# Attention and a mixture of experts on one core: the maximum pass taken in two row halves of the array, with its maxima over two banks

## The chip, the cores and the metric

The kernel runs on one core of a Trainium2 chip. The metric is the device time of one execution in microseconds (us), a median over runs. Fewer is better.

## The reference, cut to what matters

```python
# x: (1, 2048, 256), ctx: (1, 1601, 256), lenS2: the number of valid keys (at most 1601)
x = x + attention(layernorm(x), ctx, ctx, lenS2, ...)   # 16 heads of width 64, then Wo
x = x + experts(layernorm(x), gate_w, w1, w2, w3)       # 8 experts, the best 2 of each row

def attention(...):
    q_in, k_in, v_in = layer_norm(query), layer_norm(key), layer_norm(value)   # gain and bias
    q, k, v = q_in @ Wq + bq, k_in @ Wk + bk, v_in @ Wv + bv                   # 16 heads
    q, k = rope(q), rope(k)
    scores = einsum('bhqd,bhkd->bhqk', q, k) / 8
    scores = where(key < lenS2, scores, -inf)
    attn = softmax(scores)
    return einsum('bhqk,bhkd->bhqd', attn, v) @ Wo + bo
```

Everything is float32. The kernel gets near to that with bfloat16 matmuls by splitting operands into a high half (the value rounded or cut to bfloat16) and a low half (what is left).

## The kernel before

There are three stages: `prepare` (norms, transposes, splits), `attend` (the attention of the 16 heads), and `experts`. Only `attend` and constants that it uses are touched.

`attend` is compiled for 10, 11, 12 or 13 tiles of 128 keys (`KEY_TILES`) and chooses by the length at run time. In the runs here it is 10 tiles, 1280 keys: 640 exponentials over 64 blocks. `Plan(10)` sets what follows.

Two heads make a pair, and there are 8 pairs. A head's 2048 queries are 4 chunks of 512, so a pair has 8 blocks (head, chunk). A block has 5 groups of two key tiles, and the program advances in slots, one group each (`slot` on every engine; `s = 5 * block + m`).

For a head, `Q1` holds the high half of q twice (partitions 0 to 63 and 64 to 127), `K1` the high half of k on partitions 0 to 63 and its low half on 64 to 127. `Q2` holds the low half of q and on partition 64 minus the row maxima; `K2` the high half of k and on partition 64 ones. So K1 by Q1 plus K2 by Q2 (lines 682 and 683) are scores less a maximum for each query, keys on the output's partitions. ScalarE takes the exponentials (829). VectorE (974, groups 0, 2, 4) or GpSimd (1106, groups 1, 3) makes their low halves. TensorE multiplies both halves by the values, 120 matmuls of 64 or 65 columns a block (727 to 729), two slots later, and sums over a block in one bank of `pv`; two banks alternate between blocks. ScalarE copies the sums out (`copy_out`, 835) in slot m = 1 of the next block, VectorE inverts the last column (979), GpSimd multiplies (1121), and SyncE stores.

The maximum that each query needs is found one block ahead, in a pass of its own, the maximum pass. TensorE multiplies a tile of 128 queries of Q1 by 427 keys of K1 (`part`, 687, its matmul at 700) into one of three banks of `mx`; VectorE reduces those 427 columns to one (`part`, 960, at 962). 4 query tiles by 3 thirds are 12 such parts a block. `parts_of` spreads them over the slots: 3 in m = 3, then 2, 2, 3, 2 in m = 4, 0, 1, 2. In slot m = 2 VectorE reduces the three thirds to a column (`max_column`, 965). In slot m = 3 four matmuls with that column as weights turn it into a row (`max_row`, 704, at 708, into bank 0 of `mx`), and ScalarE writes it, negated, to `Q2` (841).

Within a slot TensorE does: in m = 3 the row matmuls, the scores, the parts, the products with the values; in other slots one part, the scores (4 matmuls of 512 columns), the other parts, the products (24 matmuls). The projections of the next pair (`project`, lines 640 and 645, "hooks") stand behind the slots m = 0 and m = 2 of a pair's blocks 1 to 6, 11 units of work. A block without one is called plain here.

Order between engines is by semaphores: `need(eng, sem, ...)` waits for a count. TensorE waits for `part_read` before it writes a bank of `mx` again, for `row_made` (of the block before) ahead of part (0, 0), and for `o_copied` two blocks back ahead of a block's products. Ahead of the pairs stands a first part: VectorE sets the ones of `K2` (1043), GpSimd splits Wo (1155, 1157) and then makes the rotary products of the first pair (1147), which wait for DMAs that swap halves of `q32`.

Of the kernel before, what the change touches and what calls it, by code (L numbers as in the profile page):

```python
# [17 lines left out]
P = 128  # L18
F32 = mybir.dt.float32
BF16 = mybir.dt.bfloat16  # L20
I32 = mybir.dt.int32
# [19 lines left out]
VW = 2 * HD + 1  # L41
BLOCKS = 2 * CH
# [488 lines left out]
def attend(nc, sem, maker, have):  # L531
# [9 lines left out]
    with ExitStack() as ctx:  # L541
# [3 lines left out]
        Q2 = [sb(f"Q2_{a}", [HD + 1, S], BF16) for a in range(2)]  # L545
        K1 = [sb(f"K1_{a}", [P, LP], BF16) for a in range(2)]
        K2 = [sb(f"K2_{a}", [HD + 1, LP], BF16) for a in range(2)]
# [12 lines left out]
        part_max = sb("part_max", [P, 2, QT, 3])  # L560
# [7 lines left out]
        pv = pb("pv", [P, 2, 512])  # L568
        mx = pb("mx", [P, 3, 512])
# [12 lines left out]
        ones_made = sem("ones_made")  # L582
# [14 lines left out]
        first_banks = [pj, sc[0], sc[1], pv[:, 0, :]]  # L597
# [23 lines left out]
        with nc.Block() as block:  # L621
            @block.tensor
            def _(pe):
                def program(pl):
# [60 lines left out]
                    def part(p, b_, qt, h):  # L685
# [10 lines left out]
                        if qt == 0 and h == 0:  # L696
                            need(pe, row_made, p, BLOCKS, b_)
                        need(pe, part_read, p, BLOCKS * pl.block_parts, pl.block_parts * b_ + len(pl.parts) * qt + h + 1)
                        for bank, k0 in zip(pl.part_banks(qt, h), pl.parts[h]):
                            ins = pe.matmul(mx[:, bank, 0:pl.width], Q1[a][:, c * QC + qt * P:c * QC + (qt + 1) * P],  # L700
                                            K1[a][:, k0:k0 + pl.width], start=True, stop=True)
                        ins.then_inc(part_ready, 1)

                    def max_row(p, b_):

                        need(pe, col_made, p, BLOCKS, b_ + 1)
                        for qt in range(QT):
                            ins = pe.matmul(mx[0:1, 0, qt * P:(qt + 1) * P], max_col[:, qt:qt + 1], ident_b[:], start=True, stop=True)
                        ins.then_inc(row_ready, 1)

                    def times_v(p, s):
# [10 lines left out]
                        for j, (n, t) in enumerate(pl.tiles_of(s)):  # L722
                            hi = hi_half(prob[:, s % PRING, j, :])
                            for qt in range(QT):
                                out = pv[:, i % 2, qt * (HD + 1):(qt + 1) * (HD + 1)]
# [52 lines left out]
            def _(act):  # L778
                def program(pl):
# [51 lines left out]
                    def copy_out(p, i):  # L831

                        need(act, pv_done, p, BLOCKS * pl.groups, pl.groups * (i + 1) + PRING)
                        need(act, o_made, p, BLOCKS, i + 1)
                        act.activation(o_raw[:, i % 2, :, :].rearrange("p t v -> p (t v)"), pv[:, i % 2, 0:QT * (HD + 1)],
                                       ACT.Copy).then_inc(o_copied, 1)
# [30 lines left out]
                    act.sem_inc(o_copied, 2)  # L867
# [54 lines left out]
                    act.activation(exp_ready[:], key_bias[:, 0:1], ACT.Exp)  # L922
                    max_row(0, 0)
# [9 lines left out]
            def _(dve):  # L933
                def program(pl):
# [42 lines left out]
                    def inverse(p, i):  # L977
                        need(dve, o_copied, p, BLOCKS, i + 1 + 2)
# [63 lines left out]
                    for a in range(2):  # L1042
                        dve.memset(K2[a][HD:HD + 1, :], 1.0).then_inc(ones_made, 1)
# [33 lines left out]
            def _(pool):  # L1077
                def program(pl):
# [51 lines left out]

                    def pair(p, last):
                        for s in range(LAG, BLOCKS * pl.groups + LAG):
                            slot(p, s, last)
                            if not last:
                                if s == pl.split_slot(p):
                                    split_weights(p + 1, 1)
                                for k in range(pl.units + 2):
                                    if s == pl.hook_slot(k):
                                        hooks(p + 1, k, 1)

# [31 lines left out]
            def _(sp):  # L1172
                def program(pl):
# [20 lines left out]
                    def load_q(pair, a):  # L1194
# [5 lines left out]
                        sp.dma_start(Q2[a][0:HD, :], next_lo[0][r, :]).then_inc(q_loaded[a], 16)  # L1200

                    def load_k(pair, a):
# [5 lines left out]
                        sp.dma_start(K2[a][0:HD, 0:n], next_hi[1][r, 0:n]).then_inc(k_loaded[a], 16)  # L1208
# [56 lines left out]
                    def first_load_k():  # L1265
# [4 lines left out]
                        sp.dma_start(K2[0][0:HD, 0:n], next_hi[1][0:HD, 0:n]).then_inc(k_loaded[0], 16)  # L1270

                    def first_load_q(chunks, loaded):
# [4 lines left out]
                        sp.dma_start(Q2[0][0:HD, q], next_lo[0][0:HD, q]).then_inc(loaded, 16)  # L1277
# [768 lines left out]
```

## Time and profile before

| what | value |
|---|---|
| time of three runs | 1206.67, 1209.41, 1213.72 us, median 1209.41 |
| span of the profiled execution | 1211.3 us |
| its own device time | not told apart; its span lies inside the three runs |
| TensorE (PE) busy | 1070.4 us, 88% |
| VectorE (DVE) busy | 979.4 us, 81% |
| ScalarE (ACT) busy | 731.4 us, 60% |
| GpSimd (POOL) busy | 644.6 us, 53% |
| attention, about 90 to 895 us | PE busy 9 tenths or more in each slice, DVE 9 in nearly each |

A slice is one fortieth of the span. Matmuls overlap in the pipeline, so a matmul's length in the profile is more than its place in the stream: the distance from one start to the next is what it costs. Some matmul records are missing. `PEld` are weight loads, which run beside matmuls. In a shape such as `65*128 65x512` the first pair is partitions by columns of the weights, the second of the moving operand.

### The profile page before, as it was taken

What the parts mean: (1) busy time and instruction counts of PE and PEld (TensorE: products, weight loads), DVE (VectorE), ACT (ScalarE), POOL (GpSimd) and SP (SyncE); (2) the same over time, 40 slices, a digit from 0 to 9 for tenths busy, and PEclk for the clock granted to TensorE, in tenths of its full rate; (3) what the DMA queues carried; (4) which work ended last, traced back from release to release, by engine and by line L of the source; (5) the groups of instructions that cost most, each with busy time, mean ns of one, the idle gap of its engine ahead of it and who ended that gap; (6) DMA issues with size and microseconds to landing.
All of it is one profiled execution on the core that took longest, in us unless ns stands there. A gap on an engine that the chain in (4) does not pass through costs nothing. (4 is left out here: it accounts for less than half of the span.)

```text
span 1211.3 us, 32849 instructions
## 1 busy us (share of the span) xinstructions
PE 1070.4 (88%) x12843; PEld 709.2 (59%) x13030; DVE 979.4 (81%) x1769; ACT 731.4 (60%) x1298; POOL 644.6 (53%) x457
## 2 busy tenths in 40 slices
PE   1468999999999999999999999999969958999995
PEld 1334566566656656656665665666648944566663
DVE  5878999999999999999999999999944674455552
ACT  2635666666666666666666666766644643455552
POOL 1045764674585477467448647733449554333333
PEclk9679999999999999999999999999988979999998
DMA  8034242332423324143242433317526522333330
GB/s 280 0 97 115 79 107 63 98 91 69 107 79 97 96 81 104 51 122 84 77 99 76 110 79 90 79 38 224 207 99 231 174 84 84 57 52 57 54 60 12
DMA packets 104445, 117.01 MB, mean 97 GB/s; under 512 B 47389, under 2 KB 86494, under 8 KB 103006
## 3 DMA queue, kind: packets, MB, share of 16 engines
q1 hardware_dynamic: 91214, 99.74, 29.5%
q0 software_dynamic: 7152, 8.43, 4.2%
q10 hardware_dynamic: 5920, 6.65, 2.0%
q8 instruction: 108, 1.77, 0.6%
q14 instruction: 51, 0.42, 0.1%
HBM read 39.46 MB, written 36.87 MB: 63 GB/s over the span
## 5 line engine op out<-in xcount | busy, mean ns | idle before, releaser
L829 ACT ACTIVATE prob<-sc,key_bias 128x512 f32<-128x512 f32 x640 | 405.3, 684 | 149.2 <-PE sc L683 145.1
L962 DVE TENSOR_REDUCE part_max<-mx 128x1 f32<-128x427 f32 x768 | 417.3, 590 | 35.8 <-PE mx L700 35.8
L1106 POOL TENSOR_TENSOR prob_lo<-prob 128x1024 bf16<-128x1024 f32 x128 | 242.5, 1894 | 229.4 <-ACT prob L829 229.3
L974 DVE TENSOR_TENSOR prob_lo<-prob 128x1024 bf16<-128x1024 f32 x192 | 278.2, 1449 | 9.8 <-ACT prob L829 6.2
L727 PE MATMUL pv<-VV,prob 128*128 128x65 bf16 x2560 | 267.9, 193 | 3.7 <-POOL prob_lo L1106 3.5
L729 PE MATMUL pv<-VV,prob_lo 128*128 128x65 bf16 x2560 | 269.3, 195 | 0.0
L728 PE MATMUL pv<-VV,prob 128*128 128x64 bf16 x2560 | 268.0, 193 | 0.0
L727 PEld LDWEIGHTS pv<-VV,prob 128*128 128x128 bf16 x2560 | 239.8, 99 | 38.8 <-POOL prob_lo L1106 7.3
L728 PEld LDWEIGHTS pv<-VV,prob 128*128 128x128 bf16 x2560 | 237.2, 97 | 26.4
L683 PE MATMUL sc<-Q,K 65*128 65x512 bf16 x640 | 243.6, 381 | 10.3 <-issue 4.0
L700 PE MATMUL mx<-K,Q 128*128 128x427 bf16 x768 | 236.6, 349 | 9.7 <-DVE part_max L962 5.1
L729 PEld LDWEIGHTS pv<-VV,prob_lo 128*128 128x128 bf16 x2560 | 237.4, 97 | 0.0
L682 PE MATMUL sc<-Q,K 128*128 128x512 bf16 x495 | 188.6, 381 | 0.0
L700 PEld LDWEIGHTS mx<-K,Q 128*128 128x128 bf16 x768 | 72.6, 98 | 89.5 <-DVE part_max L962 17.8
L1623 POOL DMA_INDIRECT out<-y_out,x_in x39 | 61.1, 1566 | 117.5 <-DMA out<-y_out,x_in 96.3
L1935 PE MATMUL ot<-we,xT 128*128 x443 | 112.2, 386 | 4.1 <-DVE xT L1791 1.7
L1087 POOL TENSOR_TENSOR by_sin<-q32s,we 128x512 f32<-128x512 f32 (+1 forms) x56 | 98.5, 1759 | 19.1 <-DMA q32s<-q 19.1
L683 PEld LDWEIGHTS sc<-Q,K 65*128 65x128 bf16 x640 | 62.7, 98 | 58.9 <-issue 0.3
L682 PEld LDWEIGHTS sc<-Q,K 128*128 128x128 bf16 x640 | 62.7, 98 | 49.4 <-ACT prob L829 2.6
L1100 POOL TENSOR_TENSOR we<-turned,we 128x512 bf16<-128x512 f32 (+1 forms) x56 | 55.2, 986 | 58.8 <-ACT we L804 58.8
L1935 PEld LDWEIGHTS ot<-we,xT 128*128 128x128 bf16 x468 | 43.4, 96 | 45.0 <-issue 3.7
L640 PE MATMUL pj<-we 128*128 128x320 bf16 (+1 forms) x322 | 65.1, 337 | 2.1 <-issue 1.3
(208 smaller groups left out, 1470.8 us busy)
## 6 DMA issues: line engine op xcount, KB each, us to landing
expert_inputs<-zeros SPq DMA_DIRECT2D x129, 129.0 KB, 2.8
we<-in_w_exp SPq DMA_DIRECT2D x8, 1536.0 KB, 7.9
Q<-we SPq DMA_DIRECT2D x45, 256.0 KB, 3.8
attention_out<-o_out SPq DMA_DIRECT2D x64, 128.0 KB, 2.0
o_in<-attention_out SPq DMA_DIRECT2D x16, 512.0 KB, 3.7
q32s<-q SPq DMA_DIRECT2D x122, 64.0 KB, 2.0
K<-we SPq DMA_DIRECT2D x48, 160.0 KB, 3.9
VV<-next_v SPq DMA_DIRECT2D x16, 322.5 KB, 4.0
```

Of the source, the lines that this page charges most:

```text
L682: pe.matmul(sc[n % 2][:], K1[a][:, k], Q1[a][:, q], start=True, stop=False)
L683: pe.matmul(sc[n % 2][:], K2[a][:, k], Q2[a][:, q], start=False, stop=True).then_inc(scores_ready, 1)
L700: ins = pe.matmul(mx[:, bank, 0:pl.width], Q1[a][:, c * QC + qt * P:c * QC + (qt + 1) * P], K1[a][:, k0:k0 + pl.width], start=True, stop=True)
L727: pe.matmul(out, hi_q, VV[a][:, t, HD:VW], start=t == 0 and qt == 0, stop=False, skip_group_check=True)
L728: pe.matmul(out[:, 0:HD], hi_q, VV[a][:, t, 0:HD], start=False, stop=False, skip_group_check=True)
L729: ins = pe.matmul(out, prob_lo[:, s % PRING, j, qt * P:(qt + 1) * P], VV[a][:, t, HD:VW], start=False, stop=t == pl.kt - 1, skip_group_che ...
L829: act.activation(prob[:, s % PRING, j, :], sc[n % 2][:], ACT.Exp, bias=key_bias[:, t:t + 1], scale=HD ** -0.5).then_inc(exp_done, 1)
L962: dve.tensor_reduce(part_max[:, b_ % 2, qt, h:h + 1], mx[:, pl.part_banks(qt, h)[0]:pl.part_banks(qt, h)[-1] + 1, 0:pl.width], mybir.AxisL ...
L974: dve.tensor_tensor(prob_lo[:, s % PRING, 0:g, :], prob[:, s % PRING, 0:g, :], hi_half(prob[:, s % PRING, 0:g, :])[:, :, 1::2], ALU.subtra ...
L1087: pool.tensor_tensor(by_sin[:, 0:n], q32s[:, u % 4, 0:n], (ropeq, ropek)[kind][:, 1, cols], ALU.mult).then_inc(sin_done, 1)
L1106: pool.tensor_tensor(prob_lo[:, s % PRING, 0:g, :], prob[:, s % PRING, 0:g, :], hi_half(prob[:, s % PRING, 0:g, :])[:, :, 1::2], ALU.subtr ...
L1935: ins = pe.matmul((p1, p3)[which][:], xT[:, i % 2, h, d, :], w[:, bass.ds(expert, 1), at:at + FF].rearrange("p a c -> p (a c)"), start=n = ...
```

## The change

- The maximum pass contracts over 64 partitions in place of 128, the high halves alone. Each part is now two matmuls of 320 keys, one on partitions 0 to 63 (Q1, K1), one on 64 to 127 (Q1, K2), into two banks. `mx` has 4 banks, two slots of two. 4 query tiles by 2 halves are 8 parts a block, in m = 3, 4, 0, 1, 2: 2, 2, 1, 2, 1. VectorE reduces 2 x 320 elements in one instruction.
- So that the high half of k stands on partitions 64 to 127 of `K2`, `Q2` and `K2` are turned over: the low half of q and the high half of k on 64 to 127; minus the maxima on partition 0 of `Q2`, zeros on 1 to 63; ones on 0 to 63 of `K2`. The second score matmul contracts over 128 partitions, not 65.
- The row of maxima goes to bank 3 of `mx`, and the wait for `row_made` to part (0, 1).
- The sums of the values use one bank of `pv`, not two: TensorE waits for the copy of the block just before.
- The split of Wo leaves GpSimd's start and comes in 4 pieces (2 instructions each) into the last slot of blocks 2 to 5 of the first pair. GpSimd clears `Q2` at the start, and VectorE's fill of `K2` covers 64 partitions, as 832 words.

```diff
-        if kt * P <= 3 * 512:
-            self.width = -(-kt * P // 3)
-            self.parts = [[min(j * self.width, kt * P - self.width)] for j in range(3)]
-            self.part_slots = 3
-        else:
-            self.width = -(-L // 4)
-            self.parts = [[2 * h * self.width, (2 * h + 1) * self.width] for h in range(2)]
-            self.part_slots = 1
+        self.width = -(-min(kt * P, L) // 4)
+        self.parts = [[2 * h * self.width, (2 * h + 1) * self.width] for h in range(2)]
+        self.part_slots = 2
...
-        pv = pb("pv", [P, 2, 512])
-        mx = pb("mx", [P, 3, 512])
+        pv = pb("pv", [P, 512])
+        mx = pb("mx", [P, 4, 512])
...
-                        if qt == 0 and h == 0:
+                        if qt == 0 and h == 1:
                             need(pe, row_made, p, BLOCKS, b_)
...
-                        for bank, k0 in zip(pl.part_banks(qt, h), pl.parts[h]):
-                            ins = pe.matmul(mx[:, bank, 0:pl.width], Q1[a][:, c * QC + qt * P:c * QC + (qt + 1) * P],
-                                            K1[a][:, k0:k0 + pl.width], start=True, stop=True)
+                        q = slice(c * QC + qt * P, c * QC + (qt + 1) * P)
+                        for bank, k0, rows, keys in zip(pl.part_banks(qt, h), pl.parts[h], (slice(0, HD), slice(HD, P)), (K1, K2)):
+                            ins = pe.matmul(mx[:, bank, 0:pl.width], Q1[a][rows, q], keys[a][rows, k0:k0 + pl.width], start=True, stop=True)
...
-                            ins = pe.matmul(mx[0:1, 0, qt * P:(qt + 1) * P], max_col[:, qt:qt + 1], ident_b[:], start=True, stop=True)
+                            ins = pe.matmul(mx[0:1, 3, qt * P:(qt + 1) * P], max_col[:, qt:qt + 1], ident_b[:], start=True, stop=True)
...
-                        act.activation(Q2[a][HD:HD + 1, c * QC:(c + 1) * QC], mx[0:1, 0, :], ACT.Copy, scale=-1.0).then_inc(row_made, 1)
+                        act.activation(Q2[a][0:1, c * QC:(c + 1) * QC], mx[0:1, 3, :], ACT.Copy, scale=-1.0).then_inc(row_made, 1)
...
-                    act.sem_inc(o_copied, 2)
+                    act.sem_inc(o_copied, 1)
...
-                        dve.memset(K2[a][HD:HD + 1, :], 1.0).then_inc(ones_made, 1)
+                        dve.memset(K2[a][0:HD, :].bitcast(I32), ONES_PAIR).then_inc(ones_made, 1)
...
+                    def split_wo(k):
+                        j = slice(2 * k, 2 * k + 2)
+                        pool.tensor_copy(wo_hi[:, j, :], wo32[:, j, :]).then_inc(wo_hi_made, 1)
+                        pool.wait_ge(wo_hi_made, k + 1)
+                        pool.tensor_tensor(wo_lo[:, j, :], wo32[:, j, :], wo_hi[:, j, :], ALU.subtract)
...
-                    pool.tensor_copy(wo_hi[:], wo32[:]).then_inc(wo_hi_made, 1)
-                    pool.wait_ge(wo_hi_made, 1)
-                    pool.tensor_tensor(wo_lo[:], wo32[:], wo_hi[:], ALU.subtract)
+                    for a in range(2):
+                        pool.memset(Q2[a][0:HD, :].bitcast(I32), 0).then_inc(rows_cleared, 1)
...
-                        sp.dma_start(K2[a][0:HD, 0:n], next_hi[1][r, 0:n]).then_inc(k_loaded[a], 16)
+                        sp.dma_start(K2[a][HD:P, 0:n], next_hi[1][r, 0:n]).then_inc(k_loaded[a], 16)
```

## Rows read from the trace of the kernel before

**Rows 1.** Busy by engine (instructions) in one stretch, then granted clock, DMA share, GB/s.
```profile
98.00:880.00 782.00, 743.44 (x10245) 486.10 (x10401) 739.05 (x1179) 527.18 (x903) 474.70 (x332) 1.00 0.37 98
```

**Rows 2.** The row matmuls of the whole span: min/median/max ns, first and last start.
```profile
L708 PE MATMUL mx<-ident_b,max_col x256: 217/218/311, 90.0 to 884.0; 128*1 128x128 bf16 x128
```

**Rows 3.** Waits from 98 to 880 us: waiting, waited for, us in total, times, longest.
```profile
POOL prob_lo L1106 <- ACT prob L829: 219.8, 72, 5.2
...
DVE part_max L962 <- PE mx L700: 34.2, 76, 1.4
...
PE mx L708 <- DVE max_col L968: 19.8, 41, 1.3
```

**Rows 4.** TensorE over one plain block: start us, length us, what [idle before it].
```profile
500.53 0.38 PE L708 MATMUL mx<-ident_b,max_col 128*1 128x128 bf16 x4 [0.15 <-DVE max_col L968]
...
501.29 0.38 PE L682 MATMUL sc<-Q,K 128*128 128x512 bf16 x1
501.51 0.38 PE L683 MATMUL sc<-Q,K 65*128 65x512 bf16 x1
501.73 0.71 PE L700 MATMUL mx<-K,Q 128*128 128x427 bf16 x3
...
504.99 0.34 PE L700 MATMUL mx<-K,Q 128*128 128x427 bf16 x1
...
508.92 0.19 PE L727 MATMUL pv<-VV,prob 128*128 128x65 bf16 x1
508.95 0.19 PE L728 MATMUL pv<-VV,prob 128*128 128x64 bf16 x1
...
509.13 0.36 PE L700 MATMUL mx<-K,Q 128*128 128x427 bf16 x1
...
510.19 0.34 PE L700 MATMUL mx<-K,Q 128*128 128x427 bf16 x1
510.38 0.19 PE L727 MATMUL pv<-VV,prob 128*128 128x65 bf16 x1
...
511.08 0.20 PE L729 MATMUL pv<-VV,prob_lo 128*128 128x65 bf16 x1
511.44 0.38 PE L708 MATMUL mx<-ident_b,max_col 128*1 128x128 bf16 x4 [0.16 <-DVE max_col L968]
```

**Rows 5.** Weight loads behind the row matmuls at 500.53.
```profile
500.84 0.10 PEld L682 LDWEIGHTS sc<-Q,K 128*128 128x128 bf16 x1
500.85 0.10 PEld L683 LDWEIGHTS sc<-Q,K 65*128 65x128 bf16 x1
```

**Rows 6.** TensorE where a projection stands right ahead of the row matmuls.
```profile
462.70 0.98 PE L640 MATMUL pj<-we 128*128 128x320 bf16 x6
463.61 0.38 PE L708 MATMUL mx<-ident_b,max_col 128*1 128x128 bf16 x4
```

**Rows 7.** Groups by line and shape, 100 to 870 us: busy us, mean ns.
```profile
L640 PE MATMUL pj<-we 128*128 128x320 bf16 x168 | 27.3, 299 | 0.0
```

**Rows 8.** VectorE over the same plain block.
```profile
502.11 2.13 DVE L962 TENSOR_REDUCE part_max<-mx 128x1 f32<-128x427 f32 x4 [0.29 <-PE mx L700]
504.45 0.60 DVE L962 TENSOR_REDUCE part_max<-mx 128x1 f32<-128x427 f32 x1 [0.21 <-PE mx L700]
...
511.21 0.17 DVE L968 TENSOR_REDUCE max_col<-part_max 128x4 bf16<-128x12 f32 x1
```

**Rows 9.** ScalarE: the copy of the sums of the values.
```profile
509.31 0.39 ACT L835 ACTIVATE o_raw<-pv 128x260 f32<-128x260 f32 x1 [0.21 <-PE pv L729]
```

**Rows 10.** GpSimd, then VectorE, at the start of the attention stage.
```profile
59.20 1.89 POOL L1155 CAST wo_hi<-we 128x2048 bf16<-128x2048 f32 x1 [35.45 <-issue]
61.18 4.06 POOL L1157 TENSOR_TENSOR wo_lo<-we,wo_hi 128x2048 bf16<-128x2048 f32 x1
65.21 0.86 POOL L1147 TENSOR_TENSOR by_sin<-q32s,we 128x320 f32<-128x320 f32 x1
...
62.88 0.55 DVE L1015 SCALAR_TENSOR_TENSOR by_cos<-pj,bqk,we 128x320 f32<-128x320 f32 x1
```

More of the change, by code:

```diff
@@ L41 @@
 VW = 2 * HD + 1
+WO_PARTS = H * HD // P // 2
+ONES_PAIR = 0x3F803F80
 BLOCKS = 2 * CH
@@ L544, in attend @@
         Q1 = [sb(f"Q1_{a}", [P, S], BF16) for a in range(2)]
-        Q2 = [sb(f"Q2_{a}", [HD + 1, S], BF16) for a in range(2)]
+        Q2 = [sb(f"Q2_{a}", [P, S], BF16) for a in range(2)]
         K1 = [sb(f"K1_{a}", [P, LP], BF16) for a in range(2)]
-        K2 = [sb(f"K2_{a}", [HD + 1, LP], BF16) for a in range(2)]
+        K2 = [sb(f"K2_{a}", [P, LP], BF16) for a in range(2)]
         VV = [sb(f"VV_{a}", [P, KT, VW], BF16) for a in range(2)]
@@ L559, in attend @@
         prob_lo = sb("prob_lo", [P, PRING, 2, QC], BF16)
-        part_max = sb("part_max", [P, 2, QT, 3])
+        part_max = sb("part_max", [P, 2, QT, 2])
         max_col = sb("max_col", [P, QT], BF16)
@@ L581, in attend @@
         v_loaded = [sem("v_loaded0"), sem("v_loaded1")]
-        ones_made = sem("ones_made")
+        ones_made, rows_cleared = sem("ones_made"), sem("rows_cleared")
         wo_hi_made = sem("wo_hi_made")
@@ L596, in attend @@
         first_q_loaded = [sem("first_q_loaded0"), sem("first_q_loaded1")]
-        first_banks = [pj, sc[0], sc[1], pv[:, 0, :]]
+        first_banks = [pj, sc[0], sc[1], pv]
         def first_turned(eng, m):
@@ L724, in times_v @@
                             for qt in range(QT):
-                                out = pv[:, i % 2, qt * (HD + 1):(qt + 1) * (HD + 1)]
+                                out = pv[:, qt * (HD + 1):(qt + 1) * (HD + 1)]
                                 hi_q = hi[:, 2 * qt * P + 1:2 * (qt + 1) * P:2]
@@ L834, in copy_out @@
                         need(act, o_made, p, BLOCKS, i + 1)
-                        act.activation(o_raw[:, i % 2, :, :].rearrange("p t v -> p (t v)"), pv[:, i % 2, 0:QT * (HD + 1)],
+                        act.activation(o_raw[:, i % 2, :, :].rearrange("p t v -> p (t v)"), pv[:, 0:QT * (HD + 1)],
                                        ACT.Copy).then_inc(o_copied, 1)
@@ L922, in program @@
                     act.activation(exp_ready[:], key_bias[:, 0:1], ACT.Exp)
+                    act.wait_ge(rows_cleared, 2)
                     max_row(0, 0)
@@ L977, in inverse @@
                     def inverse(p, i):
-                        need(dve, o_copied, p, BLOCKS, i + 1 + 2)
+                        need(dve, o_copied, p, BLOCKS, i + 1 + 1)
                         dve.reciprocal(rden[:, i % 2, :], o_raw[:, i % 2, :, HD]).then_inc(rden_made, 1)
@@ L1139, in pair @@
                                         hooks(p + 1, k, 1)
+                            if p == 0 and s % pl.groups == pl.groups - 1 and 2 <= s // pl.groups < 2 + WO_PARTS:
+                                split_wo(s // pl.groups - 2)
                     pool.sem_inc(o_made, 2)
@@ L1199, in load_q @@
                         sp.dma_start(Q1[a][HD:P, :], next_hi[0][r, :]).then_inc(q_loaded[a], 16)
-                        sp.dma_start(Q2[a][0:HD, :], next_lo[0][r, :]).then_inc(q_loaded[a], 16)
+                        sp.dma_start(Q2[a][HD:P, :], next_lo[0][r, :]).then_inc(q_loaded[a], 16)
                     def load_k(pair, a):
@@ L1269, in first_load_k @@
                         sp.dma_start(K1[0][HD:P, 0:n], next_lo[1][0:HD, 0:n]).then_inc(k_loaded[0], 16)
-                        sp.dma_start(K2[0][0:HD, 0:n], next_hi[1][0:HD, 0:n]).then_inc(k_loaded[0], 16)
+                        sp.dma_start(K2[0][HD:P, 0:n], next_hi[1][0:HD, 0:n]).then_inc(k_loaded[0], 16)
                     def first_load_q(chunks, loaded):
@@ L1276, in first_load_q @@
                         sp.dma_start(Q1[0][HD:P, q], next_hi[0][0:HD, q]).then_inc(loaded, 16)
-                        sp.dma_start(Q2[0][0:HD, q], next_lo[0][0:HD, q]).then_inc(loaded, 16)
+                        sp.dma_start(Q2[0][HD:P, q], next_lo[0][0:HD, q]).then_inc(loaded, 16)
                     for m in range(5):
```

## The prediction

> **What bounds the kernel now.** First the busy time by stretch, to see where the change acts and how full the engines are there. In the attention stage, 98 to 880 us, the granted clock is 1.00 (2.4 GHz), TensorE is busy 743.4 of 782 us and VectorE 739.1 [rows 1]. The two stand within a per cent of each other, so neither number names the bound. The reader is to see that whatever is taken from one of them alone is soon limited by the other. 64 groups of row matmuls start from 90.0 to 884.0 us, 63 steps: 12.60 us a block on average, with the projections [rows 2]. A plain block takes 500.53 to 511.44, 10.91 us [rows 4].
>
> Then the waits [rows 3]: TensorE waits for VectorE's column of maxima 41 times, 19.8 us in all; VectorE waits for the maximum matmuls 76 times, 34.2 us. GpSimd waits 219.8 us for exponentials and has room. Then TensorE in order of time, to count its work by starts, not by lengths. Score matmuls start 0.22 us apart, matmuls with the values 0.03, and a 427-column part takes 0.18 (three are 0.71 us, of which the last alone shows 0.35) [rows 4]. So a plain block is 20 x 0.218 = 4.36, 12 x 0.18 = 2.16 and 120 x 0.0303 = 3.64, 10.16 together. What is left of 10.91, 0.75, lies around the row matmuls: the last value matmul starts at 511.08, the row at 511.44. TensorE sets the pace, and gives some of it to VectorE's column of maxima once a block.
>
> One thing in these rows decides the case. Behind four row matmuls (128 moving columns on one output column, 0.38 us for four, so the last starts 0.16 after the first, at 500.69, and its columns end 0.053 later) the next weight load starts only at 500.84 [rows 4, 5]. No wait stands there, and elsewhere a weight load is pulled ahead of the running matmul. So 0.10 us are lost on going back from a one-column output to the full array. In the other direction: six projection matmuls of 320 columns span 0.98 us with 0.299 for one [rows 6, 7], so they start (0.98 - 0.30) / 5 = 0.136 apart, the last is through at 463.52, and the row starts at 463.61: 0.09. A change of the array's division costs about 0.095 us each way here.
>
> **The change part by part.** The sum is made against the profiled span, 1211.3 us, which is 1.9 above the median of the runs.
>
> *The parts themselves.* 12 x 0.18 = 2.16 us a block go. 8 pairs of 320 columns come. If both halves stream at once, a pair costs 0.136: 1.09 us. If they go one after the other, 0.272: 2.18. The trace has no two matmuls in different rows of the array; I take both at once, as that is the point of addressing half the rows, and keep 2.18 as the other end. Saving 1.07 us a block. The second of a pair starts later than the first by something between 0.01 (a full-array matmul follows its weight load by that, 500.84 and 500.85) and 0.03 (the spacing of value matmuls [rows 4]); it is exposed once for each run of parts, 7 a block: 7 x 0.02 = +0.14.
>
> The Trainium skill, "TensorE: Matmul & The Clock Gate", Part 3, says that matmuls in different row groups run together, starting about 4 ns apart. By that the +0.14 would be +0.03, an estimate; no run here shows it yet.
>
> *Changes of division.* In m = 3 the two parts stand together, in m = 4 and 1 one stands ahead of the scores and one behind, in m = 0 and 2 one ahead: 7 runs of parts, each with a change before and after, 14 a block. The bounds: 0, if halving rows is not like narrowing columns, and 0.165, the whole latency of a matmul (0.195 long, 0.03 apart). The nearest row is the 0.095 of the row matmuls, and I take it: 14 x 0.095 = +1.33 us a block. The row matmuls' own two changes stay.
>
> The Trainium skill, "TensorEngine Tiling (Array Packing)", Tiling Modes, says under Key Properties that changing the tiling mode, not just the tile, drains the engine, and gives no figure. The 0.10 and 0.09 above agree with it. It is the rule that speaks against this change: with it the sum is near nothing, without it a clear gain.
>
> *VectorE.* Reductions of 427 start 0.51 us apart ((2.13 - 0.60) / 3) [rows 8]. 213 more elements at 0.96 per ns are 0.22: 0.73 for 640. 8 x 0.73 = 5.86 against 12 x 0.51 = 6.14: -0.28 us a block of VectorE, nothing of it on the path while TensorE sets the pace. Crossing a bank I cost at nothing; at 0.06 each it would be +0.5, still hidden then.
>
> *TensorE's wait for the column.* Now a part stands directly ahead of the last products (510.19, then 510.38 [rows 4]) and VectorE reads it while they run. After the change slot m = 2 has one part, ahead of its scores, 0.87 us earlier. The 41 waits are 19.8 us beyond the modelled ends, each some 0.07 more by starts: 22.7 us in 60 blocks, 0.38 a block. With VectorE also 0.28 lighter I take 0.30 of it as gone; ends 0 and 0.38.
>
> *One bank for the sums.* TensorE's first products of a block wait for the copy. It ends at 509.70 (509.31 + 0.39) [rows 9]; the products start at 510.38 now and would at about 510.3. Slack 0.6 us: nothing. The cover is the four score matmuls of slot m = 2. Without it the price is at most the copy, 0.39 a block, 25 us; behind the waiting product on TensorE would stand everything, and VectorE behind that.
>
> *The rest.* The second score matmul over 128 partitions, not 65: both kinds start 0.22 apart [rows 4], nothing. DMAs: the same number and bytes to other partitions, nothing. Row in bank 3, wait at part (0, 1): the scores, 0.87 us, now stand between row and that wait in slot m = 3, nothing, at most 0.05 gained. At the start the split of Wo, 1.89 + 4.06 us, goes from GpSimd, whose first rotary product followed it directly at 65.21 [rows 10]; two clears of 1024 words, under 1.9 each, come. VectorE's fills get shorter. But later products wait for the swaps, so of at most 1.1 us I take 0.5. The split's four pieces, 1.5 us each, lie in GpSimd's 219.8 us of waiting [rows 3]; uncovered, 6 us.
>
> Sum a block: -1.07 + 0.14 + 1.33 - 0.30 = +0.10; by 64: +6.4 us. With the start 1211.3 + 6.4 - 0.5 = 1217.2; less 1.9 against the median: **1215 us**, some 0.5% slower.
>
> **The rivals.**
>
> *The changes of division cost little, and VectorE becomes the bound (A).* For it: halving rows uses all output columns, and the row matmuls' loss may belong to their one-column weights. Against it: the load behind them has the usual form and is late all the same. Below about 0.03 us a change, TensorE needs 12.60 - 0.38 - 1.07 + 0.14 + 0.4 = 11.7 us a block or less. VectorE is busy 739 us in 62 blocks, 11.9, less 0.28: 11.64. With half of its present idle time, 0.35, it is 12.0 a block, -0.6: 64 x 0.6 = 38, so 1211.3 - 38 - 0.5 - 1.9 = 1171 us. It decides below 0.03 us a change; from there the gain falls, to nothing at 0.088 (1.33 - 0.10, over 14).
>
> *The changes cost more, or part of the overlap is missing (D).* At 0.165: 14 x 0.07 = +0.98 a block, +63 us: 1278; at 0.13, +31: 1246. For it: a part of 320 columns has to leave the array before the scores' weights go in, and the way back has two loads. Against it: the two measured changes are 0.09 and 0.10.
>
> *The halves go one after the other (C),* the change not doing what it says: +1.09 a block, +70 us: 1285. Against it: nothing in the addresses makes one wait for the other, banks and rows differ.
>
> **How the numbers follow.** Forecast (changes at 0.07 to 0.11 us) 0.42, own range 1200 to 1230. A 0.33, 1155 to 1190, and 0.03 between the two. D 0.14, C 0.08. The sign is uncertain and both sides have weight, so the range reaches over both: 1163 to 1262, leaving A's lower fifth, C and the upper part of D outside. A difference under 0.5% (6 us) is what a measurement of this kernel can't tell from none. Faster: A 0.33, the 0.03 between and 0.04 of the forecast, 0.40. Same (1203.4 to 1215.5): 0.19, all from the forecast. Slower: 0.19 of the forecast, D 0.14, C 0.08, 0.41.
>
> **What would show it.** Starts of TensorE around a part: from a value matmul to the first half 0.12 rather than 0.04, from the second half to the scores 0.23 rather than 0.14. The two halves' starts 0.01 to 0.03 apart (0.136: C). Reductions 0.73 apart. VectorE's waits for the maximum matmuls up from 34 towards 60 us, TensorE's for the column down from 19.8 to under 8; in A the first falls, and TensorE waits for `part_max`. No wait of the products for the copy. Steps of the row matmuls: 12.7 us (A: 12.0; D, C: 13.2 and more). If VectorE's reductions over two banks take 0.9 us or more, the sum is wrong at another place.

## The result, and the profile after

The changed kernel takes 1232.3 us (median of 4 runs, 1231.3 to 1235.4), the kernel before 1211.1 in the same comparison: ratio 1.018, 95% interval 1.015 to 1.021. It is 21 us slower. The forecast was 1215, 0.5% slower, in a range of 1163 to 1262. The result lies in that range, but above the part of it, 1200 to 1230, that belonged to the forecast itself and not to a rival. One run of the experiments below, of 4764 us in before_behind, is left out of its median and ratio.

The page of the changed kernel, and its row matmuls over the span (the columns are those of [rows 2]):

```profile
span 1229.5 us, 33115 instructions
...
PE 1068.8 (87%) x13099; PEld 674.2 (55%) x13286; DVE 972.2 (79%) x1513; ACT 726.3 (59%) x1298; POOL 647.1 (53%) x465
```

```profile
L705 PE MATMUL mx<-ident_b,max_col x256: 217/218/311, 89.6 to 906.4; 128*1 128x128 bf16 x128
```

The 63 steps from the first row matmul to the last are 816.8 us, 12.97 each, against 794.0 and 12.60 before [rows 2]: 22.8 us, so all of the loss is in the blocks of attention, none in the experts. The first row comes 0.4 us earlier. What follows the last row, untouched by the change, took 323.1 us here and 327.3 before; it varies from 323.1 to 330.0 over the traces of this case, which is why the two spans lie only 18.2 us apart. Steps of the row matmuls are the steadier measure.

Groups by line and shape, 100 to 880 us of the changed kernel (busy us, mean ns of one | idle before it and what ended most of it):

```profile
L960 DVE TENSOR_REDUCE part_max<-mx 128x1 f32<-128x640 f32 x479 | 377.8, 815 | 29.7 <-PE mx L698 27.7
...
L698 PE MATMUL mx<-K,Q 64*128 64x320 bf16 x956 | 137.7, 305 | 17.4 <-DVE part_max L960 17.2
```

Then TensorE in order of time around one slot's two parts, m = 1 (to be read beside [rows 4]):

```profile
509.50 0.19 PE L725 MATMUL pv<-VV,prob 128*128 128x64 bf16 x1
509.53 0.20 PE L726 MATMUL pv<-VV,prob_lo 128*128 128x65 bf16 x1
509.66 0.31 PE L698 MATMUL mx<-K,Q 64*128 64x320 bf16 x2
...
510.34 0.38 PE L679 MATMUL sc<-Q,K 128*128 128x512 bf16 x1
510.56 0.38 PE L680 MATMUL sc<-Q,K 128*128 128x512 bf16 x1
510.87 0.31 PE L698 MATMUL mx<-K,Q 64*128 64x320 bf16 x2
511.11 0.20 PE L724 MATMUL pv<-VV,prob 128*128 128x65 bf16 x1
```

The halves do run at once: the two matmuls of a part are one entry of 0.31 us, as long as one alone (mean 0.305); in the trace their starts lie 0.003 us apart. And the changes of division are there, at the size of the row matmuls' [rows 4 to 6]: from the last value matmul to the part 0.13 where 0.03 is the spacing; from the part to the next products 0.24 where its columns take 0.136; from the last scores to the part 0.31 where 0.22 is the spacing. Each is 0.09 to 0.10 more.

And where a plain block ends, to be read beside 511.08 and 511.44 of [rows 4]:

```profile
513.79 0.20 PE L726 MATMUL pv<-VV,prob_lo 128*128 128x65 bf16 x1
513.92 0.38 PE L705 MATMUL mx<-ident_b,max_col 128*1 128x128 bf16 x4
```

From the last value matmul to the row matmuls it is 0.13, where it was 0.36: in a plain block TensorE does not wait for the column of maxima any more, and 0.23 us are saved. The parts cost 0.33 more (2.49 us in place of 2.16, worked out further down). Together that is 0.10, and a plain block grew by 0.11, from 10.91 to 11.02. So in plain blocks the prediction's sum (+0.10) came true, with both terms 0.07 smaller than put (0.40 and 0.30). Most of the loss is elsewhere.

Waits from 98 to 880 us, the changed kernel, then the kernel before:

```profile
ACT prob L826 <- PE sc L680: 194.9, 236, 2.3
...
DVE part_max L960 <- PE mx L698: 27.7, 59, 1.5
...
PE mx L698 <- DVE part_max L960: 17.4, 31, 1.2
...
PE mx L705 <- DVE max_col L966: 13.3, 14, 1.6
```

```profile
ACT prob L829 <- PE sc L683: 141.8, 211, 1.3
...
PE mx L700 <- DVE part_max L962: 2.5, 8, 0.8
```

TensorE waits less for the column of maxima (13.3 us, before 19.8 [rows 3]) but 17.4 us for a free slot of `mx`, where it was 2.5. The reader is to see the second number: it is a wait that the prediction did not have. By step of a pair (the table below has the eight steps): of the 19.8 us before, 14.5 lay in the third and fourth step and 5.4 in all others; after the change all 14 waits, 13.3 us, are in the third and fourth, and so are 15.4 of the 17.4 us for a slot. ScalarE's wait for scores went from 142 to 195 us. Some of that only shows that the steps are longer, the rest that scores come late behind a full slot.

The starts of ScalarE's copy of the row (line 841 before, 838 after) give a block's length. From the second pair on (in four_slots from the third) a pair's pattern repeats to 0.03 us, but for one step of before_two_slots (14.72 in the fourth pair, not 13.36) and two of before_no_part_in_m2 (11.44 for 11.20, 14.45 for 14.36). One such pair, its eight steps and its length, then a step of the last pair, which has no projections:

| kernel | steps of the second or a later pair, us | pair | plain |
|---|---|---|---|
| before | 10.90 13.64 14.12 14.35 12.61 14.13 11.58 10.97 | 102.3 | 10.91 |
| after | 11.02 13.88 14.74 15.63 13.02 14.18 11.57 11.03 | 105.1 | 11.02 |
| full_rows | 10.95 13.55 14.75 15.62 12.66 14.30 11.30 10.95 | 104.1 | 10.95 |
| together_ahead | 11.61 14.25 14.75 15.62 13.18 14.08 11.79 11.45 | 106.7 | 11.61 |
| together_behind | 10.92 13.44 13.87 14.73 12.35 14.04 11.36 10.92 | 101.6 | 10.92 |
| lone_behind | 11.36 13.88 13.87 14.73 13.02 14.05 11.80 11.36 | 104.1 | 11.36 |
| same_half | 12.06 14.94 15.02 15.34 13.82 14.87 12.50 12.07 | 110.6 | 12.06 |
| before_two_slots | 12.52 14.36 15.04 15.45 13.36 14.74 12.53 12.57 | 110.6 | 12.51 |
| one_pv_bank | 10.91 13.63 14.11 14.34 12.61 14.13 11.57 10.97 | 102.3 | 10.91 |
| four_slots | 10.91 13.64 14.11 14.34 12.52 14.23 11.57 10.96 | 102.3 | 10.90 |
| before_behind | 11.21 13.64 13.94 14.34 12.53 14.04 11.75 11.26 | 102.7 | 11.21 |
| no_part_in_m2 | 10.73 13.46 14.48 14.32 12.29 13.18 10.87 10.73 | 100.0 | 10.73 |
| before_no_part_in_m2 | 10.94 13.72 14.91 14.36 12.87 13.57 11.20 10.99 | 102.5 | 10.94 |

Of the 2.8 us that a pair is longer after the change, 1.9 are in two steps, the third and fourth. A plain block is only 0.11 longer. The first pair is not in the table: it took 108.9 us after the change and 103.4 before, 5.5 more, 2.1 of them in those two steps. So of the 22.8 us, 13.5 are in the third and fourth steps of the seven pairs with projections, 3.4 in the other steps of the first pair, and 6 are spread over the rest. In the third step TensorE shows this:

```profile
437.22 0.31 PE L698 MATMUL mx<-K,Q 64*128 64x320 bf16 x2
...
439.20 0.31 PE L698 MATMUL mx<-K,Q 64*128 64x320 bf16 x2 [0.82 <-DVE part_max L960]
...
439.89 0.38 PE L679 MATMUL sc<-Q,K 128*128 128x512 bf16 x1
```

VectorE and ScalarE over the same time:

```profile
435.13 1.56 DVE L960 TENSOR_REDUCE part_max<-mx 128x1 f32<-128x640 f32 x2 [1.34 <-PE mx L698]
436.60 0.74 DVE L938 SCALAR_TENSOR_TENSOR by_cos<-pj,bqk,we 128x512 f32<-128x512 f32 x1
437.26 1.15 DVE L947 TENSOR_TENSOR turned<-by_cos,by_sin 128x512 f32<-128x512 f32 x1
438.34 1.54 DVE L960 TENSOR_REDUCE part_max<-mx 128x1 f32<-128x640 f32 x2
```

```profile
436.95 1.27 ACT L826 ACTIVATE prob<-sc,key_bias 128x512 f32<-128x512 f32 x2 [1.06 <-PE sc L680]
440.15 1.27 ACT L826 ACTIVATE prob<-sc,key_bias 128x512 f32<-128x512 f32 x2 [1.93 <-PE sc L680]
```

The part at 439.20 stands ahead of the scores of slot m = 0. Both slots of `mx` are full. VectorE has still to read both, but the projection's cosines and turn (436.60 to 438.34) stand ahead of these two reductions. The first of the two has to be over, at 439.1, before TensorE may write. Nothing else on TensorE may pass: the scores wait behind the part, and ScalarE waits 1.93 us for the scores.

The fourth step has one thing more. Here it is in the changed kernel, the kernel before and lone_behind (an experiment below); the columns are those of [rows 1], the third engine is VectorE:

```profile
448.51:464.13 15.62, 12.52 (x170) 7.45 (x172) 15.15 (x18) 9.57 (x17) 11.21 (x8) 1.00 0.26 72
```

```profile
436.90:451.25 14.35, 12.65 (x167) 8.00 (x170) 14.31 (x22) 9.40 (x16) 11.51 (x8) 1.00 0.27 78
```

```profile
442.86:457.59 14.73, 12.84 (x173) 7.18 (x173) 14.70 (x18) 9.60 (x17) 11.90 (x8) 1.00 0.28 76
```

VectorE is busy 15.15 of 15.62 us, and was busy 14.31 of 14.35 already before the change. Of its idle time after the change 0.43 us are one wait for ScalarE's copy of the sums (over 98 to 880 us 16.7, before 2.6). So in this step VectorE, with next to no idle time, sets the length, and not TensorE, in both kernels. Its reductions take less than before (6.5 us in place of 7.1), but the two `turned` take 3.6 us in place of 2.95 and the three `prob_lo` 4.5 in place of 4.3. The same instruction on the same 512 columns has another length with another order of work: the mean of `turned` is 1370 ns before, 1568 after, 1122 in no_part_in_m2. Why is not shown here.

### The profile page after: what moved, and what is told of

Same layout as the page of the kernel before. It is cut to its first block and busy times, and to the rows that moved or that the text cites. A ratio compares the mean times of both kernels' runs of the same rounds, so it can differ in the third digit from the quotient of the medians.

```text
span 1229.5 us, 33115 instructions
## 1 busy us (share of the span) xinstructions
PE 1068.8 (87%) x13099; PEld 674.2 (55%) x13286; DVE 972.2 (79%) x1513; ACT 726.3 (59%) x1298; POOL 647.1 (53%) x465
## 5 line engine op out<-in xcount | busy, mean ns | idle before, releaser
L960 DVE TENSOR_REDUCE part_max<-mx 128x1 f32<-128x640 f32 x512 | 403.2, 815 | 30.2 <-PE mx L698 28.1
L724 PE MATMUL pv<-VV,prob 128*128 128x65 bf16 x2560 | 270.7, 194 | 2.8 <-POOL prob_lo L1104 2.6
L680 PE MATMUL sc<-Q,K 128*128 128x512 bf16 x640 | 243.6, 381 | 22.8 <-issue 20.2
L725 PEld LDWEIGHTS pv<-VV,prob 128*128 128x128 bf16 x2560 | 238.2, 97 | 14.5
L679 PE MATMUL sc<-Q,K 128*128 128x512 bf16 x495 | 190.1, 384 | 0.0
L698 PE MATMUL mx<-K,Q 64*128 64x320 bf16 x1024 | 149.6, 309 | 27.5 <-DVE part_max L960 24.1
L698 PEld LDWEIGHTS mx<-K,Q 64*128 64x128 bf16 x1024 | 44.5, 93 | 137.6 <-issue 87.1
L1098 POOL TENSOR_TENSOR we<-turned,we 128x512 bf16<-128x512 f32 (+1 forms) x56 | 71.4, 1275 | 79.3 <-ACT we L801 79.3
L679 PEld LDWEIGHTS sc<-Q,K 128*128 128x128 bf16 x640 | 62.0, 97 | 83.9 <-ACT prob L826 2.4
L1085 POOL TENSOR_TENSOR by_sin<-q32s,we 128x512 f32<-128x512 f32 (+1 forms) x56 | 78.8, 1407 | 9.2 <-DMA q32s<-q 9.2
L680 PEld LDWEIGHTS sc<-Q,K 128*128 128x128 bf16 x640 | 63.0, 98 | 37.3 <-issue 0.5
```

What stands on the lines that cost most here:

```text
L679: pe.matmul(sc[n % 2][:], K1[a][:, k], Q1[a][:, q], start=True, stop=False)
L680: pe.matmul(sc[n % 2][:], K2[a][:, k], Q2[a][:, q], start=False, stop=True).then_inc(scores_ready, 1)
L698: ins = pe.matmul(mx[:, bank, 0:pl.width], Q1[a][rows, q], keys[a][rows, k0:k0 + pl.width], start=True, stop=True)
L724: pe.matmul(out, hi_q, VV[a][:, t, HD:VW], start=t == 0 and qt == 0, stop=False, skip_group_check=True)
L725: pe.matmul(out[:, 0:HD], hi_q, VV[a][:, t, 0:HD], start=False, stop=False, skip_group_check=True)
L960: dve.tensor_reduce(part_max[:, b_ % 2, qt, h:h + 1], mx[:, pl.part_banks(qt, h)[0]:pl.part_banks(qt, h)[-1] + 1, 0:pl.width], mybir.AxisL ...
```

## The experiments

Ratios are to the kernel before, run on the same chip beside each. Each expectation names theories by a letter. T: the changes of division cost the time. V: VectorE, the coarser slots and the one bank of sums cost it.

**full_rows: no changes of division.**

```diff
-  ... (slice(0, HD), slice(HD, P)), (K1, K2)):
+  ... (slice(0, P), slice(0, P)), (K1, K1)):
```

> The changed kernel with each of its 320-key matmuls on all 128 partitions (Q1 by K1) again: two a part, one after the other, no change of the array's division. Everything else of the change stays (maxima of 640 over two banks, four banks of mx in two slots, one bank of sums, row in bank 3, split of Wo in pieces). Theory T (the changes of division, 14 a block at 0.095 to 0.10 us, eat the overlap of the halves): parts cost 16 x 0.136 = 2.18 us a block and not 7 x 0.335 + 0.14 = 2.49, so TensorE has 0.31 less, 20 us over 64 blocks: 1212 us, or a little less where the waits shrink too. Rival V (the coarser slots of mx, VectorE's reductions and the one bank of sums cost the time): stays at 1225 to 1235. Under V more columns in the stream make it slower still, up to 1240.

1228.0 us, ratio 1.012 (1.009 to 1.015). First a part among scores and value matmuls without the halves, from its trace:

```profile
456.48 0.43 PE L698 MATMUL mx<-K,Q 128*128 128x320 bf16 x2
456.76 0.19 PE L724 MATMUL pv<-VV,prob 128*128 128x65 bf16 x1
...
457.46 0.20 PE L726 MATMUL pv<-VV,prob_lo 128*128 128x65 bf16 x1
457.49 0.43 PE L698 MATMUL mx<-K,Q 128*128 128x320 bf16 x2
```

The products start 0.28 after the part, the two times 0.136 that its columns take, and a part starts 0.03 after the last value matmul. The 0.10 us each way are gone: they belong to the halves, not to the place of the part. Then its row matmuls, a part that waits in a third step, and its waits:

```profile
L705 PE MATMUL mx<-ident_b,max_col x256: 217/218/311, 90.3 to 900.3; 128*1 128x128 bf16 x128
```

```profile
450.26 0.43 PE L698 MATMUL mx<-K,Q 128*128 128x320 bf16 x2
...
452.65 0.45 PE L698 MATMUL mx<-K,Q 128*128 128x320 bf16 x2 [1.21 <-DVE part_max L960]
```

```profile
PE mx L705 <- DVE max_col L966: 16.1, 14, 1.8
PE mx L698 <- DVE part_max L960: 15.9, 19, 1.2
```

The steps are 810.0 us together, 6.8 less than after the change, where T alone wanted 20. The time lies in V's span (1225 to 1235) and 16 us over T's, though it fell and V gave no reason for a fall. This is the run to remember: without any change of division and without any overlap 16.0 of the 22.8 us are still lost against the kernel before. In a plain block (10.95) the 14 changes, 1.4 us, and the overlap cancel to 0.31 in its favour, but two of its parts now start 0.11 and 0.30 us after the value matmul ahead of them, not 0.03: 0.34 us of waiting for a slot in place of the 0.31. The table says where the rest sits: steps three and four are 14.75 and 15.62, the same as with the halves, and here too the part of m = 0 waits 1.21 us. A third theory comes from this, R: two slots of `mx` are too few for parts that stand ahead of scores.

**together_ahead and together_behind: where the parts stand.**

```diff
 # together_ahead
-                            if n == 0 and not behind:
+                            if n == len(pl.parts_of(s)) - 1 and not behind:
                                 slot_scores(p, s, last)
 # together_behind: in every slot, ahead of the loop over the parts
+                        if not behind:
+                            slot_scores(p, s, last)
...
-                            if n == 0 and not behind:
-                                slot_scores(p, s, last)
```

> The changed kernel with the parts of a slot all ahead of its scores: in slots m = 4 and 1 both parts stand in one run, 5 runs a block in place of 7, so 4 changes of division fewer. T: each run less saves 0.095 + 0.24 - 0.14 = 0.195 us, 2 a block, 25 us over 64 blocks as an upper bound: 1207 to 1220. Against that the second part of a run is asked for before VectorE has read a slot, and TensorE's wait for part_max (17.4 us now) grows. Rival V: that growth is all that happens, 1235 to 1250.

1248.4 us, ratio 1.030 (1.026 to 1.034), in V's span, 28 us over T's. The two runs fewer brought nothing that shows; the wait for a slot more than doubled:

```profile
PE mx L698 <- DVE part_max L960: 38.6, 102, 0.8
```

> As together_ahead, but the parts of each slot stand behind its scores and ahead of the products with the values, in all slots. 5 runs of parts a block again. T: up to 25 us faster than the changed kernel, 1207 to 1220. The scores come 0.3 us earlier for ScalarE. V: no gain, since VectorE gets its parts later and the column of maxima in slot m = 2 is late by 0.9 us: TensorE's wait for max_col goes up from 13 to 30 us or more, 1235 to 1250.

1209.6 us, ratio 0.996 (0.995 to 0.998): 2.1% faster than the changed kernel (by the two ratios), and a shade faster than before. This is T's span, and V is wrong here. Its waits:

```profile
PE mx L705 <- DVE max_col L966: 22.3, 41, 1.5
...
PE mx L698 <- DVE part_max L960: 7.2, 15, 0.8
```

Both orders have 5 runs of parts and 10 changes of division; they lie 39 us apart. So the place of a part is worth more than the change of division beside it.

**same_half: both matmuls of a part in partitions 0 to 63.**

```diff
-  ... (slice(0, HD), slice(HD, P)), (K1, K2)):
+  ... (slice(0, HD), slice(0, HD)), (K1, K1)):
```

> The changed kernel with both matmuls of a part in the same row half (partitions 0 to 63, Q1 by K1): the changes of division stay, the overlap goes. T and the trace of the changed kernel (both halves start together, a pair takes 0.14): a pair takes 0.27, +0.136 x 8 = 1.09 us a block, 70 us over 64 blocks, less what is in waits now (30 us): 1272 to 1302. V (TensorE is not the bound): 1232 to 1250.

1278.6 us, ratio 1.054 (1.051 to 1.057), 46 us over the changed kernel (43 by the steps of the row matmuls), in T's span. One part and a run of two on TensorE:

```profile
504.62 0.44 PE L698 MATMUL mx<-K,Q 64*128 64x320 bf16 x2
...
510.55 0.71 PE L698 MATMUL mx<-K,Q 64*128 64x320 bf16 x4
```

0.44 for two and 0.71 for four in place of 0.31 and 0.45: one after the other, 0.135 apart. A plain block is 1.04 us longer, as 8 x 0.135 = 1.08 asks. Over all blocks it is less than T gave (70 us before waits), since in steps three and four (+0.28, -0.29) TensorE had been waiting anyway.

**lone_behind: only the single parts of m = 0 and m = 2 behind their scores.**

```diff
+                        lone = len(pl.parts_of(s)) == 1
+                        if lone:
+                            slot_scores(p, s, last)
...
-                            if n == 0 and not behind:
+                            if n == 0 and not behind and not lone:
```

> The changed kernel, but the single part of slots m = 0 and m = 2 stands behind its slot's scores, not ahead. 7 runs of parts and 14 changes of division a block as in the changed kernel. Theory R (ring): the two slots of mx are full when VectorE is held by the projection's work (cosines and turn, 2.2 us), and the part that stands ahead of the scores in m = 0 then holds the scores back; full_rows shows TensorE waiting 1.2 us there. R: with the part behind, the scores go on, and most of what together_behind gained (22 us over the changed kernel) comes: 1212 to 1222. Theory T (the changes of division alone): same count, so 1230 to 1236.

1228.0 us, ratio 1.013 (1.011 to 1.014), between the spans of R and T, nearer to T's. TensorE in a third step: the part of m = 0 (434.43) now behind scores that start at 433.44 without a wait. Then its waits:

```profile
432.45 0.31 PE L698 MATMUL mx<-K,Q 64*128 64x320 bf16 x2
...
433.44 0.38 PE L679 MATMUL sc<-Q,K 128*128 128x512 bf16 x1
...
434.43 0.31 PE L698 MATMUL mx<-K,Q 64*128 64x320 bf16 x2
...
435.43 0.38 PE L637 MATMUL pj<-we 128*128 128x512 bf16 x1
```

```profile
PE mx L705 <- DVE max_col L969: 20.0, 40, 1.5
...
PE mx L698 <- DVE part_max L963: 5.3, 22, 0.4
```

With the changes of division as many as before, steps three and four fall from 14.74 and 15.63 to 13.87 and 14.73, which are those of together_behind to the digit: 1.77 us a pair, 12 us over 7 pairs. That shows R for these two steps as far as the part's place goes; that `turned` is shorter here in the fourth step too (3.1 us for two, 3.6 after the change) is a part of it that this run does not separate. What kept the total up is a cost that R did not price: the part of m = 2 comes later, so the column of maxima does, TensorE waits 20.0 us for it again (13.3), and a plain block goes from 11.02 to 11.36. There the row matmuls start 0.47 us after the last value matmul, not 0.13: the whole 0.34.

From lone_behind to together_behind a plain block loses 0.44: two runs of parts fewer, by the timeline 2 x (0.10 + 0.10) = 0.40. In both the row waits alike (0.47 after the last value matmul), so this is the changes of division seen where nothing hides them.

**before_two_slots.**

```diff
-            self.part_slots = 3
+            self.part_slots = 2
```

> The kernel before with two of its three banks of mx in use: 427-key parts on all rows, two banks of sums, nothing else changed. R: the depth of the ring is what the projection blocks need, so the blocks that took 14.1 and 14.35 us go towards 14.8 and 15.6, some 2 us a pair and more since a slot now holds only 427 columns: 1225 to 1245. T: the ring plays no part, 1211 to 1216.

1285.2 us, ratio 1.061 (1.058 to 1.063). Its waits:

```profile
DVE part_max L962 <- PE mx L700: 65.5, 126, 1.5
PE mx L700 <- DVE part_max L962: 46.1, 92, 0.7
...
PE mx L708 <- DVE max_col L968: 20.3, 35, 1.5
```

46.1 us of waiting for a slot in place of 2.5. The ring's depth matters, with nothing else changed. It is worth more than I gave it (40 us above R's span): here a slot holds 427 columns, not 640, and plain blocks wait as well (12.51). That the smaller slot is the reason was not tried by itself.

**one_pv_bank and four_slots.**

```diff
 # one_pv_bank, in the kernel before (its other lines only follow the new shape and count)
-        pv = pb("pv", [P, 2, 512])
+        pv = pb("pv", [P, 512])
...
-                    act.sem_inc(o_copied, 2)
+                    act.sem_inc(o_copied, 1)
 # four_slots: the same, and
-            self.part_slots = 3
+            self.part_slots = 4
-        mx = pb("mx", [P, 3, 512])
+        mx = pb("mx", [P, 4, 512])
```

> The kernel before with one bank for the sums of the values in place of two. Both theories hold that the copy (0.39 us) is over before the next block's products: 1211 to 1217. A third view, that the single bank costs part of the 21 us: 1220 to 1235 (0.39 us a block at most, 25 us).

1212.3 us, ratio 1.000 (0.998 to 1.001). The single bank costs nothing in the kernel before, and all its steps are those of before. In the changed kernel no wait of TensorE's value matmuls for the copy shows either.

> The kernel before with one bank for the sums and the bank that this frees as a fourth slot of mx: 427-key parts on all rows. R: the waits of the projection blocks fall further (TensorE's for part_max and max_col, 22 us before), 1195 to 1210. T: no change, 1211 to 1217.

1213.9 us, ratio 1.000 (0.998 to 1.002). A miss for R's forecast of a gain: with parts of 427 columns three slots are enough, and a fourth brings nothing.

**before_behind, no_part_in_m2, before_no_part_in_m2: does the change pay in another order?**

```diff
 # parts behind the scores as in together_behind, and for the last two
+        if self.groups == 5:
+            each = [self.block_parts // 4] * 4 + [0]
```

> The kernel before with all parts of a slot behind its scores (as together_behind has them), nothing of the change. If the order alone was what together_behind gained over the changed kernel (22 us), it should help here too: 1195 to 1208. Theory R with its ring of three slots: the ring is deep enough here and seldom holds the scores, so the order brings nothing there, while the last two parts of m = 2 now come 0.87 us later and the column of maxima with them: 1213 to 1235.

1219.6 us, ratio 1.005 (1.003 to 1.007), in R's span. The order alone does not help the kernel before; its wait for the column rose from 19.8 us:

```profile
PE mx L708 <- DVE max_col L968: 30.1, 41, 1.7
```

> together_behind with the 8 parts as 2, 2, 2, 2, 0 over slots m = 3, 4, 0, 1, 2: 4 runs of parts a block, 8 changes of division, and VectorE has all parts a slot before the column is due. T: one run less saves 0.195 us a block, 12 us. Column theory: together_behind still waits 22 us for the column of maxima, most of which goes. Together 1175 to 1195. If VectorE's own work (11.6 to 12 us a block with the projections) is the bound by then, it stops at 1190 to 1205.

1198.0 us, ratio 0.988 (0.985 to 0.991). The fastest order, 15 us under the kernel before. Its row matmuls, and what is left of its waits for VectorE:

```profile
L707 PE MATMUL mx<-ident_b,max_col x256: 217/218/311, 90.1 to 868.9; 128*1 128x128 bf16 x128
```

```profile
PE mx L700 <- DVE part_max L962: 10.7, 28, 0.5
...
PEld mx L707 <- DVE max_col L968: 5.2, 26, 0.3
```

TensorE no longer shows a wait of its own for the column, only its weight loads do, 5.2 us. It stopped above the span of T and the column theory together and inside the one for VectorE's work being the bound. That VectorE's work is the bound does not follow: it still waits 47.6 us for parts here. What does bound it was not separated.

> The kernel before with its 12 parts as 3, 3, 3, 3, 0, behind the scores: full array, three slots, no change of division. The column wait (20 us) should go as in no_part_in_m2: 1190 to 1208. Three parts in a row fill the ring just ahead of the products; where VectorE is behind, the third waits and holds the products back, then 1205 to 1220. Against no_part_in_m2 TensorE's stream is 2.16 for the parts and not 4 x 0.335 + 4 x 0.14 = 1.90: the row halves should win by up to 0.26 us a block, 17 us.

1215.3 us, ratio 1.002 (1.000 to 1.003). In the same order the kernel before gains nothing, though its wait for the column fell from 19.8 to 3.8 us; why is open. The changed kernel wins by 1.4% here (0.988 to 1.002), 17 us. That is the whole change, not the row halves alone: VectorE's 8 reductions of 0.73 us are also 0.28 us a block less than 12 of 0.51, 18 us over 64 blocks if none of it were hidden. An edit like full_rows in this order would tell the two apart; none was run.

**no_part_in_m2_wo: the split of Wo at the start.**

```diff
# beside the order of no_part_in_m2; the pieces in the first pair's blocks go
+                    for k in range(WO_PARTS):
+                        split_wo(k)
```

> no_part_in_m2 with the split of Wo back at GpSimd's start (behind the clears of Q2), none of it in the first pair's blocks. The first pair of no_part_in_m2 takes 103.0 us where the later ones take 100.0, and 2.0 of that lie in one block (15.2 against 13.2) right behind pieces of the split; the kernel before lost 1.1 in its first pair. If the pieces cost it: the first pair falls to 101, and the start gains nothing, since its first products wait for the swap DMAs: 1194 to 1197. If the split at the start costs what it costs in GpSimd (6 us on the path there): 1200 to 1203.

1197.4 us, ratio 0.987 (0.985 to 0.989), the same time. Both costs are there and cancel: the first pair fell from 103.0 to 101.0 us, and the first row came 2.5 us later (93.2 against 90.8).

## Why the prediction was right, and where not

The direction held, and so did the mechanism in plain blocks: no gain, because the array's changes of division cost more than the overlap saves, and most of that comes back from TensorE's wait for the column (+0.33 - 0.23 there, +0.11 measured). But most of the 21 us has another cause, which the sum put at nothing: the two-slot ring in the blocks with projections. full_rows, without a change of division, still loses 16.0 of 22.8 us. That the result stays inside the range owes something to luck: the range was drawn wide for two rivals, and the time, 1232, lies between the forecast's own span (up to 1230) and D's times (from 1246).

- *Halves at once, 0.136 a pair, the second 0.02 late.* Right in the pair; the 0.02, in all 0.14 a block, was too much: the second starts 0.003 after the first.
- *14 changes at 0.095.* Right in size, 0.09 to 0.10 each way. The parts take 8 x 0.136 + 14 x 0.10 = 2.49 us of the stream against 2.16: +0.33 a block where I had +0.40. But a change that falls into a wait costs nothing: without all 14 (and without the overlap) the steps fell by 0.11 us a block (full_rows), not by 0.31.
- *VectorE 0.73 a reduction over two banks.* Right (1.54 to 1.56 for two, so 0.73 to 0.74 apart). Crossing the bank costs nothing that shows: one of 640 takes 815 ns and one of 427 took 590 (225 more for 213 elements).
- *TensorE's wait for the column, -0.30 a block.* This step failed. It spread an average evenly over the blocks. In plain blocks the wait went wholly (0.23 us by starts). But 14.5 of the 19.8 us lay in the third and fourth steps, where VectorE has the projections' work, and 13.3 stay there: the wait fell by 6.5 us, not by 19.
- *The ring of `mx`, not in the sum at all.* This failed too: 17.4 us of waiting for a slot came where 2.5 were. The sum treated the ring only as banks. It went from three slots to two, and a slot is now held until 640 columns are read. That projections stand in blocks 1 to 6 and that parts stand ahead of scores was known; the two were not put together. lone_behind gives the size: 1.77 us in two of a pair's steps, 12 us of the 21, or of the 17 between forecast and result. TensorE's two waits together rose by 8.4 us where the sum had -19; with the parts' 21 that would be 29 us against 22.8 measured, so such terms do not simply add, and the rest is not told apart step by step.
- *"TensorE sets the pace".* True in plain blocks. In the fourth step of a pair VectorE did, before the change (busy 14.31 of 14.35 us) and after (15.15 of 15.62); the averages of [rows 1] hide it.
- *One bank for the sums, nothing.* Right (one_pv_bank).
- *Split of Wo hidden in GpSimd's waits.* Wrong in a small way: the waits are an average over all blocks. In the order of no_part_in_m2 the pieces cost 2.0 us in the first pair, and the start, 2.5 us earlier with them, gives it back; in the changed kernel's own order they were not tried.
- *The start, -0.5.* Right, -0.4.
- *Rivals.* A fell in its condition (a change costs 0.10, not under 0.03) and its time (1171), but its signs came: VectorE's waits fell (27.7 us from 34.2) and TensorE waits for `part_max`, for the reason above and in the blocks with projections. C fell, and same_half shows what it would have been (1279; I said 1285). D's size of a change fell. The signs named for the forecast were half right: starts as said; steps 12.97, not 12.7; VectorE's waits did not rise towards 60, and TensorE's for the column did not go under 8.

## What to carry to other kernels

Two matmuls in two row halves of the array do run at once here, but each change between halves and full array costs 0.1 us, so group them, and count runs, not matmuls. Do not spread an average wait over all blocks: look in which steps it lies, and which engine is busy all through them. When a change makes the pieces of a ring larger and fewer, look for the instruction of the producer that stands ahead of something urgent, and for the block in which the consumer is busy with other work: there the ring's depth is priced, not in a plain block. A change that loses can hold a gain for another order: the same halves behind the scores, in four runs, with none in m = 2, are 1.2% faster than the kernel before, and the kernel before gains nothing from that order.

## What the runs showed of the hardware

Changing between the full array and one output column, and between the full array and row halves, costs the same 0.09 to 0.10 us each way. The weight load of the value matmul behind a part starts with it (both at 511.11), where between value matmuls it starts 0.03 ahead (509.50 for the one at 509.53); whether that is a part of the 0.1 was not tried.
